# Audio tower: expert down products with w2 stationary, gate weights applied in the relu

## What is computed

```
logits = einsum('bsh,he->bse', x, gate_w) + gate_b
topk_vals, topk_idx = top_k(logits, 2)
weights = one_hot(topk_idx) weighted by softmax(topk_vals)        # [b, s, e]
h = relu(einsum('bsh,ehf->bsef', x, w1) + b1)                     # 128 -> 256
expert_out = einsum('bsef,efh->bseh', h, w2) + b2                 # 256 -> 128
return einsum('bseh,bse->bsh', expert_out, weights)
```

## Time and profile before

| | us |
|---|---|
| median of three executions | 633.38 (631.23 to 635.68) |
| the profiled execution, its time | 632.56 |
| its span, first to last instruction | 630.8 |

### The profile page before, as it was taken

How to read it: one execution, slowest core, us unless ns; L and a number is a source line. 1 busy time by engine, 2 the same in 40 slices (tenths; PEclk the granted TensorE clock), 3 DMA queues, 4 the chain that set the end, 5 groups by cost and what they waited for, 6 DMA issues and landing times. The chain is left out here.

```text
span 630.8 us, 40775 instructions
## 1 busy us (share of the span) xinstructions
PE 580.2 (92%) x17503; PEld 476.8 (76%) x17503; DVE 383.3 (61%) x1096; ACT 385.6 (61%) x783; POOL 311.6 (49%) x450
## 2 busy tenths in 40 slices
PE   1899999998899899999999999999999999989996
PEld 1587777776467788887887887887887887867774
DVE  4446666664256367588588588588588588343332
ACT  1357666676558348568668668668668668244442
POOL 2767677763167455555655655655655654100000
PEclk9979999999889799999999999999999999999999
DMA  2500000100000011011011011111011011000000
GB/s 61 146 18 11 9 8 12 28 2 2 3 3 1 21 36 42 25 35 40 26 34 53 25 37 44 32 38 38 25 50 38 25 41 38 3 13 0 13 13 13
DMA packets 26264, 17.40 MB, mean 28 GB/s; under 512 B 3020, under 2 KB 25700, under 8 KB 26212
## 3 DMA queue, kind: packets, MB, share of 16 engines
q1 hardware_dynamic: 24388, 14.11, 7.8%
q0 software_dynamic: 672, 2.12, 1.2%
q10 hardware_dynamic: 1152, 0.53, 0.3%
HBM read 15.27 MB, written 1.48 MB: 27 GB/s over the span
## 5 line engine op out<-in xcount | busy, mean ns | idle before, releaser
L458 POOL TENSOR_TENSOR T<-Q,W 128x368 f32<-128x368 f32 x192 | 182.4, 967 | 162.7 <-issue 145.4
L606 ACT ACTIVATE Q<-P 64x368 f32<-64x368 f32 x384 | 195.3, 508 | 89.0 <-DVE P L816 80.2
L948 PEld LDWEIGHTS bank<-P 46*46 46x46 f32 x6144 | 155.1, 122 | 34.1 <-issue 26.3
L948 PE MATMUL bank<-P 46*46 46x46 f32 x6144 | 168.9, 208 | 7.6 <-DVE P L816 3.2
L948 PE MATMUL bank<-W 46*46 46x46 f32 x6144 | 166.7, 208 | 0.0
L948 PEld LDWEIGHTS bank<-W 46*46 46x46 f32 x6144 | 151.1, 121 | 0.1
L806 DVE SCALAR_TENSOR_TENSOR W<-Q,bank 128x368 f32<-128x368 f32 x192 | 101.9, 531 | 27.1 <-PE bank L948 20.0
L816 DVE SCALAR_TENSOR_TENSOR P<-T,bank 128x368 f32<-128x368 f32 x160 | 85.1, 532 | 35.1 <-PE bank L948 32.6
L642 ACT ACTIVATE hT<-bank,b_sb 128x360 f32<-128x360 f32 x128 | 69.7, 559 | 54.5 <-PE bank L948 52.0
L948 PE MATMUL bank<-xnT,w1c 128*128 x168 | 61.9, 491 | 11.3 <-issue 11.3
L914 DVE SCALAR_TENSOR_TENSOR acc<-bank,wt,acc 120x128 f32<-120x128 f32 x144 | 41.6, 344 | 47.3 <-PE bank L948 47.3
(11 more groups left out here) (133 smaller groups left out, 766.7 us busy)
## 6 DMA issues: line engine op xcount, KB each, us to landing
w2c<-in_L_ffn_w SPq DMA_DIRECT2D x42, 128.0 KB
w1c<-in_L_ffn_w SPq DMA_DIRECT2D x42, 128.0 KB, 2.0
w_sb<-in_L_ffn_w POOLq DMA_DIRECT2D x2, 1024.0 KB, 7.4
pat<-in_x SPq DMA_DIRECT2D x24, 60.0 KB
out<-outb SPq DMA_DIRECT2D x24, 60.0 KB
wqkv_sb<-in_L_attn_w_qkv ACTq DMA_DIRECT2D x1, 192.0 KB, 2.7
band<-scratch SPq DMA_DIRECT2D x2, 66.1 KB
cn<-in_consts ACTq DMA_DIRECT2D x1, 72.0 KB, 1.8
```

Source lines behind the costliest of these rows:

```text
L458: pool.tensor_tensor(out=T[g], in0=Q[g], in1=W[g], op=ALU.add).then_inc(s_t[g], 1)
L606: ins = act.activation(Q[g][to, :, :], P[g][fro, :, :], ACT.Copy, scale=T_IN)
L948: return pe.matmul(out, lhsT, rhs, start=start, stop=stop, skip_group_check=True)
```

## The change

**Products.** `down` makes w2 stationary and moves the 360 tokens of `hT`: two products in place of six. The result has features on partitions. **Gate weights.** They can no longer be scalars per partition, so they are applied before the down product: `weighted` on DVE takes over from ACT's `relus` and computes max(up, -b1) times the gate weight, the weight being a row of 360 tokens spread over 128 partitions. max(up, -b1) is relu(up + b1) - b1, so b2 is corrected once, ahead of the loop, by the sum of w2 times b1 (sixteen products on PE with `bz`, an addition on DVE, eight copies on ACT). **Rows.** SP writes each block's turned weights `wT` to DRAM (`wrow`) and loads one row per step into one of three buffers `wB`, spread over all partitions (128 x 360 float32, 184 KB); the buffers are tiles of the first stage. **Accumulation.** `add_up` replaces `mix`: one instruction that adds bank 7 to the slot of `xnT` that the block before has left, so `xnT` has nine slots. **End.** In the tail, after the iterations that `ends` names, PE turns a block's sum back (`turn_back`, three transposes into bank 0 or 1), DVE adds the residual (`finish`) and ACT issues the stores, which SP did before.

```diff
-            for t in (OT[:, BT:BTP], wT[:, BT:BTP], hT[:, 0, :, :], hT[:, 1, :, BT:BTP], xnF[:, BT:BTP]):
+            for t in (OT[:, BT:BTP], wT[:, BT:BTP], hT[:, 0, :, :], hT[:, 1, :, BT:BTP], xnF[:, BT:BTP], bz[:, :, :]):
...
+        def ends(i):
+            return {54: 0, 56: 1, 58: 2, 60: 3, 62: 4, 64: 5, 72: 6}.get(i)
...
+            def weight_rows(d):
+                sp.wait_ge(s_wT, d + 1)
+                sp.dma_start(wrow[d, :, :], wT[:, 0:BT]).then_inc(s_wd, 16)
+            def row_over(q):
+                d, e = real(q)
+                sp.wait_ge(s_wd, 16 * d + 16)
+                if q - IDLE >= 3:
+                    sp.wait_ge(s_hT, 2 * (q - 3) + 4)
+                sp.dma_start(wB[q % 3], wrow[d, e, :].partition_broadcast(128)).then_inc(s_wB[q % 3], 16)
...
-            for q in range(LOOPED):
-                up_weights(q)
+            for q in range(IDLE + STEPS):
+                if q < LOOPED:
+                    up_weights(q)
                 if q < LOOPED - 1:
                     down_weights(q)
-                if q - IDLE > EXPERTS and real(q)[1] == 1:
-                    store(real(q)[0] - 1)
-            for blk in range(real(LOOPED - 2)[0], BLOCKS):
-                store(blk)
+                if q % ITERS == 0 and 0 < q // ITERS <= BLOCKS:
+                    weight_rows(q // ITERS - 1)
+                if q == IDLE:
+                    row_over(q)
+                if IDLE <= q and q + 1 < IDLE + STEPS:
+                    row_over(q + 1)
...
-            act.activation(b1_sb[:, :], bank[6][:, 0:2 * EXPERTS], ACT.Copy).then_inc(s_b1, 1)
+            act.activation(b1_sb[:, :], bank[6][:, 0:2 * EXPERTS], ACT.Copy, scale=-1.0).then_inc(s_b1, 1)
+            for e in range(EXPERTS):
+                act.activation(bz[:, 2 * e:2 * e + 2, e], bank[6][:, 2 * e:2 * e + 2], ACT.Copy).then_inc(s_bz, 1)
...
-                        if n == 1 and expert_step(i) is not None and j % 2 == (i < TAIL):
-                            relus(expert_step(i))
...
+                    if j % 2 and ends(blk * ITERS + j // 2) is not None:
+                        store(ends(blk * ITERS + j // 2))
...
+            dve.wait_ge(s_b2p, 1)
+            dve.tensor_tensor(out=b2_sb[:, :], in0=bank[4][0:EXPERTS, 0:D], in1=b2_sb[:, :], op=ALU.add).then_inc(s_b2r, 1)
             dve.wait_ge(s_band, 16 * 2)
...
-                dve.tensor_tensor(out=wt[:, blk * TILES:(blk + 1) * TILES, :], in0=em[:, :, :],
-                                  in1=every(er[:, :], EXPERTS), op=ALU.mult).then_inc(s_wt, 1)
...
-            def mix(q):
...
-                for t in range(TILES):
-                    ins = dve.scalar_tensor_tensor(out=dst[:, t, :], in0=y[:, t, :], scalar=wt[:, blk * TILES + t, e:e + 1],
-                                                   in1=before[:, t, :], op0=ALU.mult, op1=ALU.add)
-                ins.then_inc(s_mix, 1)
+            def weighted(q):
+                e = real(q)[1]
+                b = (q - LOOPED + 1) % 2 if q >= LOOPED else 0
+                dve.wait_ge(s_b1, 1)
+                dve.wait_ge(s_wB[q % 3], 16 * ((q - IDLE) // 3) + 16)
+                for f in range(2):
+                    dve.wait_ge(s_up, 2 * q + f + 1)
+                    dve.wait_ge(s_dn, q if q > LOOPED else q + 1)
+                    dve.scalar_tensor_tensor(out=hT[:, b, f, 0:BT], in0=bank[5 + f][:, 0:BT],
+                                             scalar=b1_sb[:, 2 * e + f:2 * e + f + 1], in1=wB[q % 3],
+                                             op0=ALU.max, op1=ALU.mult).then_inc(s_hT, 1)
+            def add_up(q):
+                d, e = real(q)
                 dve.wait_ge(s_dn, q + 2)
+                y = xnT[:, slot(d)]
+                if e:
                     dve.wait_ge(s_mix, q + 2)
+                    dve.tensor_tensor(out=y, in0=bank[7][:, 0:BT], in1=y, op=ALU.add).then_inc(s_mix, 1)
                 else:
+                    dve.tensor_copy(y, bank[7][:, 0:BT]).then_inc(s_mix, 1)
+            def finish(d):
+                dve.wait_ge(s_yT, d + 1)
+                wait(dve, s_out, 16 * TILES * d)
+                dve.wait_ge(s_acc, d + 1)
+                dve.tensor_tensor(out=outb[:, :, :], in0=bank[d % 2][0:TT, 0:TILES * D].rearrange("p (t d) -> p t d", t=TILES),
+                                  in1=resid[:, d * TILES:(d + 1) * TILES, :], op=ALU.add).then_inc(s_fin, 1)
...
-                        mix(expert_step(i - 1))
+                        add_up(expert_step(i - 1))
+                    if expert_step(i) is not None and j % 2 == (i < TAIL):
+                        weighted(expert_step(i))
+                    if j % 2 and ends(i) is not None:
+                        finish(ends(i))
...
+            pe.wait_ge(s_bz, EXPERTS)
+            for n in range(2 * EXPERTS):
+                ins = mm(bank[4][0:EXPERTS, 0:D], bz[:, n, :], w2_sb[:, n, :], start=(n == 0), stop=(n == 2 * EXPERTS - 1))
+            ins.then_inc(s_b2p, 1)
...
             def down(p, b, w, *ready):
                 wait_apart(pe, met, (s_hT, 2 * p + 2), (s_mix, p + 1), *ready)
-                for t in range(TILES):
-                    for f in range(2):
-                        ins = mm(bank[7][:, t * D:(t + 1) * D], hT[:, b, f, t * TT:t * TT + 128],
-                                 w[:, f, :], start=(f == 0), stop=(f == 1))
+                for f in range(2):
+                    ins = mm(bank[7][:, 0:BT], w[:, f, :], hT[:, b, f, 0:BT], start=(f == 0), stop=(f == 1))
                 ins.then_inc(s_dn, 1)
...
+            def turn_back(d):
+                wait_apart(pe, met, (s_mix, IDLE + 2 + 8 * d + 8), (s_p[d % 2], BLOCKS * ITERS))
+                wait(pe, s_fin, d - 1)
+                for t in range(TILES):
+                    ins = pe.transpose(bank[d % 2][0:TT, t * D:(t + 1) * D], xnT[:, d * BT + t * TT:d * BT + (t + 1) * TT], ident)
+                ins.then_inc(s_yT, 1)
...
+                if ends(i) is not None:
+                    turn_back(ends(i))
+            turn_back(BLOCKS - 1)
```

More of the change, by code:

```diff
@@ L228, in tower @@
         er = sb("er", [TT, TILES])
-        wt, wtF = sb("wt", [TT, BLOCKS * TILES, EXPERTS]), sb("wtF", [TT, TILES, EXPERTS])
+        wtF = sb("wtF", [TT, TILES, EXPERTS])
+        wrow = nc.dram_tensor("wrow", (BLOCKS, EXPERTS, BT), F32, kind="Internal").ap()
+        wB = [t.rearrange("p a b -> p (a b)")[:, 0:BT] for t in (E[0], E[1], X[0])]
+        bz = sb("bz", [128, 2 * EXPERTS, EXPERTS])
         wT = sb("wT", [EXPERTS, BTP])
         hT = sb("hT", [128, 2, 2, BTP])
-        acc = sb("acc", [TT, TILES, D])
         outb = sb("outb", [TT, TILES, D])
@@ L256, in tower @@
         s_r, s_o = sem("s_r"), sem("s_o")
+        s_wB = [sem(f"s_wB{i}") for i in range(3)]
+        s_wd, s_bz, s_b2p, s_b2r, s_yT, s_fin = (sem("s_wd"), sem("s_bz"), sem("s_b2p"), sem("s_b2r"),
+                                                 sem("s_yT"), sem("s_fin"))
         s_gv, s_xnF, s_wtF, s_wup, s_wdn = sem("s_gv"), sem("s_xnF"), sem("s_wtF"), sem("s_wup"), sem("s_wdn")
@@ L610, in xn_out @@
                 act.wait_ge(s_xnF, blk + 1)
-                to = (blk + 1) % BLOCKS
-                act.activation(xnT[:, to * BT:(to + 1) * BT], xnF[:, 0:BT], ACT.Copy).then_inc(s_xnT, 1)
+                act.activation(xnT[:, slot(blk + 1)], xnF[:, 0:BT], ACT.Copy).then_inc(s_xnT, 1)
             def xn_here(blk):
@@ L634, in attention_rows, with store @@
                                ACT.Copy).then_inc(s_OT, 1)
-            def relus(q):
-                e = real(q)[1]
-                b = (q - LOOPED + 1) % 2 if q >= LOOPED else 0
-                for f in range(2):
-                    act.wait_ge(s_up, 2 * q + f + 1)
-                    act.wait_ge(s_dn, q if q > LOOPED else q + 1)
-                    act.activation(hT[:, b, f, 0:BT], bank[5 + f][:, 0:BT], ACT.Relu,
-                                   bias=b1_sb[:, 2 * e + f:2 * e + f + 1]).then_inc(s_hT, 1)
+            def store(d):
+                act.wait_ge(s_fin, d + 1)
+                for t in range(TILES):
+                    dst = bass.AP(tensor=out.tensor, offset=d * (BB * NP * D) + t * (TN * D),
+                                  ap=[[NP * D, BB], [D, TN], [1, D]])
+                    act.dma_start(dst, outb[:, t, :]).then_inc(s_out, 16)
             def turned_weights(blk):
                 act.wait_ge(s_wtt, blk + 1)
+                wait(act, s_wd, 16 * blk)
                 act.activation(wT[:, 0:BT], bank[4][0:EXPERTS, 0:BT], ACT.Copy).then_inc(s_wT, 1)
```

33 lines of the change are left out of this document (9 added, 24 removed).

## The result

The changed kernel takes 625.17 us (median of four, 623.25 to 625.43) where the kernel before, run beside it, takes 633.75: a ratio of 0.988, 95% interval 0.984 to 0.992. In a second group it came to 623.96 us and 0.987 (0.984 to 0.990). It is faster by 1.2 to 1.3%, just beyond the 1% that a measurement of this kernel can tell; I had forecast 627.4, inside that 1%. The profiled execution took 623.25 us, 9.3 less than the one before, with a span of 621.4 and a mean granted clock of 0.988.

What follows compares the result with a forecast made beforehand. PE was taken to set the pace in loop and tail, except at the gate, where it waits for DVE. Setup, loop, tail, turning and end summed to -6.0 us: 626.6 profiled, 627.4 forecast as median, range 618.5 to 634.5.

Steps and rivals of the forecast that it cites:

- the wait of 0.7 us ahead of the transposes of wtF: Sign the forecast is right: in the loop, PE waits 0.7 us or so before turning wtF at the gate.
- The shorter down: Down product on PE, four records instead of twelve: 0.26 us gained per loop step, 0.19 per tail step.
- The 50 us that I set beside the sum: Alternative estimate from the Trainium skill's bf16 matmul spacing: new down at 0.61 us, gaining some 50 us over 70 steps.
- The gate's 0.80 us: Gate in each loop block: added DVE work delays wtF and the next squares, giving back 0.80 us per block.
- the norm's 0.30: Third norm in each loop block: its DVE operations now stand behind `weighted`, giving back 0.30 us.
- the rival that `weighted` itself would be slowed: Shared port, no gain: `weighted` loses time beside GpSimd at gate and norm, some 6 us, about 633; chance 0.20.
- DVE keeps up: Faster rival: waits for ACT go, nothing is given back at gate or norm, another 6.6 us, about 621; chance 0.22.
- Setup: Before the loop: sixteen products for the corrected b2 delay the first W by 0.6 us; ends nothing and 2.1.
- turning: Tail: three products turn each block back, 0.35 us each time, seven times on PE's path, +2.5 us.
- end: Last block's down, `add_up`, turning and last add: +0.3 us at the program's end.
- Rows by DMA: One 184 KB broadcast per step on SP's queue, issued one iteration ahead, hidden: cost nothing.
- The clock: Slower rival: the new wait at wtF lowers PE's granted clock in six blocks, +20 us, about 647; chance 0.08.

## Why the prediction was right, and where its steps were not

The time lay in the range and 2.2 us under the forecast. I had put it within 1% of no change, at the faster edge, and it came out just beyond. That it lay so near is in part luck: two steps that were wrong partly cancelled, and the setup came out shorter where I had it longer. Of the signs that I had named, the records of 0.30 us and the tail's steps came, the wait of 0.7 us ahead of the transposes of wtF did not.

*The shorter down* was right in kind: four records at 0.30 us. Its size in the loop was wrong: 0.13 us, not 0.26. I took the loop's 1.50 us against the up product's 1.22 in the tail, and so counted the two gaps (0.075 and 0.095 us) as part of the old form; they stay. In the tail 0.21 came where I had 0.19, of which 0.13 is the form. The 50 us that I set beside the sum were misworked: they took the old form at its measured duration and only the new one at the other rate, so they are no estimate of the change.

*The gate's 0.80 us and the norm's 0.30* were not given back. This is the step that failed. The sum carried the durations of before along: 2.35 us for the gate's second half, which held an `oh` of 0.90, and the norm's 1.84. Both lay beside a T of GpSimd, and the added 1.0 us of `weighted` moved them clear of it, or into its last 0.3 us, where the norm took its 0.34 us all the same. Take 0.72 off my chain (and put `weighted` at its measured 1.00) and it gives wtF at 7.65 and the squares at 8.8 us; measured are 7.63 and 8.82. So six blocks gave 4.5 us where I had 2.8: less from the product, nothing back. I had noticed the norm's 1.84 beside the tail's 0.85 and used it for the rival that `weighted` itself would be slowed. It was not: 587 ns on the mean beside a T and clear of it. P, W and `add_up`, which read a bank too, likewise have one duration wherever they lie; `oh`, with two inputs in SBUF, the norm and the cast are held, and end 0.03 to 0.09 us behind the T beside them. The Trainium skill (SBUF — State Buffer, SBUF: two separate sides) states it as an exclusive lock, held for the whole of an instruction, in which the later one is blocked; the traces agree, with 0.18 against 0.90 us and 0.34 against 1.01. What I had not drawn from that is that such a delay belongs to a place in time and not to an instruction.

*DVE keeps up*, the faster rival, gave 621 on the ground that the waits for ACT go. Its outcome (nothing given back) came, for another reason: `add_up` starts 1.49 us behind the down, where the sum had 1.45, so no earlier for ACT's relief, and with ACT relieved just as much the norm placed inside a T cost its block 0.4 to 0.5 us again.

*Setup.* +0.6 was too little: leaving the products out gives 3 to 4 us, of which 1.3 to 1.8 can be seen in the setup. That the profile after nevertheless reaches the first down 1.3 us earlier goes, as far as can be seen, to the clock, which fell twice between 166 and 184 us in the profile before and not there in the one after. Windows of both falls, before and after:

```profile
166.00:170.00 4.00, 4.00 (x79) 2.49 (x77) 1.08 (x2) 3.89 (x8) 0.00 (x0) 0.57 0.02 4
179.00:184.00 5.00, 5.00 (x151) 3.32 (x139) 2.56 (x6) 1.85 (x4) 1.95 (x3) 0.66 0.00 2
```

```profile
166.00:170.00 4.00, 2.99 (x75) 1.89 (x75) 1.96 (x5) 3.87 (x8) 0.00 (x0) 1.00 0.01 4
179.00:184.00 5.00, 5.00 (x239) 3.38 (x232) 2.88 (x6) 2.85 (x7) 3.56 (x4) 1.00 0.02 5
```

The granted clock is 0.57 and 0.66 before, 1.00 after. The second stretch seems to lie where nothing covers it: the kernel before with the relus on VectorE has the same setup and in its profile only the first fall, and took 39.2 us from `dprod` to the first down where the kernel before took 41.0.

*Rows by DMA, turning, end* were as priced: nothing, 0.33 for 0.35, +0.24 for +0.3. *The clock* rival did not come either: from 225 to 614 us the granted clock is 1.00.

## What to carry to other kernels

Before the cost of a moved instruction is carried over, look at what it overlaps: where one kind of instruction has two durations (0.18 and 0.90, 0.34 and 1.01), the difference belongs to its place, and a longer queue ahead of it can make it faster. Price a product from its spacing in the same surroundings, with the gaps at both its ends, rather than from the best row of another stretch. Work put ahead of a pipelined start is not free merely because the first result behind it is on time; follow the start through to the first steady period.

## What the runs showed of the hardware

In every profile PE's granted clock fell to 0.50, the 1.2 GHz level, at the entry of the first block with expert steps, between 208 and 216 us (in the changed kernel at 210 us, behind 5 us in which PE was busy for 3.4; in the kernel before at 214). How long it stayed there differed from execution to execution of one kernel. Windows of the same 19 us in the kernel before, the changed kernel, the changed kernel again, and the second profile of the one without the b2 products:

```profile
203.00:222.00 19.00, 16.84 (x577) 15.29 (x576) 6.94 (x15) 7.38 (x15) 8.97 (x10) 0.82 0.07 18
```

```profile
203.00:222.00 19.00, 16.13 (x623) 12.42 (x612) 7.39 (x15) 7.62 (x16) 8.18 (x10) 0.91 0.09 25
```

```profile
203.00:222.00 19.00, 17.29 (x526) 13.82 (x515) 6.51 (x13) 6.56 (x13) 8.17 (x10) 0.73 0.06 18
```

```profile
203.00:222.00 19.00, 16.82 (x563) 13.35 (x562) 6.79 (x14) 7.64 (x16) 6.92 (x8) 0.82 0.08 24
```

The granted clock is 0.82, 0.91, 0.73 and 0.82. From `dprod` to the end of the first block the profiles take 88.3 to 96.0 us, while the five blocks behind it repeat within 0.4 us in kernels with the same loop. So most of the spread of the times is made there, as far as one profile of each kernel shows, and that is presumably what hid two thirds of a gain in the loop of 3.4 us (the gate ahead of add_up). The mean clock listed with the runs was 0.9804 for the kernel before (59 runs) and 0.9848 for the changed one (9): over 625 us an estimate of 2.7 us. With it the account closes roughly: 7.0 us from six blocks, tail and end, 0.8 from the six shorter downs of the first block, 2.7 from the clock, less the 1.3 to 1.8 us that the b2 products cost in the setup, is 8.7 to 9.2; the medians moved by 8.6 and 8.8. Why the clock stays low for 3.4 us in one execution of the changed kernel and for 10.2 in another (up to 13.7 in the other profiles), and whether the change has a part in it, was not settled.
